# Guard rows issued by ScalarE, operand loads two to a chunk, value products dealt two-one-one, and fewer filler products

## The reference

```python
q, k, v = proj(Wq, bq), proj(Wk, bk), proj(Wv, bv)      # (16, 16 heads, 512, 8)
idx = clip(pos[None, :] - pos[:, None], -20, 20) + 20
attn1 = einsum('bhqd,bhkd->bhqk', q, k)
attn2 = einsum('bhqd,qkd->bhqk', q, rel_k[idx])
attn = softmax((attn1 + attn2) / sqrt(8), axis=-1)
w1 = einsum('bhqk,bhkd->bhqd', attn, v)
w2 = einsum('bhqk,qkd->bhqd', attn, rel_v[idx])
out = (w1 + w2) @ Wo.T + bo                              # heads merged
h = silu(norm(x) @ wg.T) * (norm(x) @ wu.T); y = x + h @ wd.T
```

## Time and profile before

| | |
|---|---|
| median of 3 runs | 1243.12 us (1238.39 to 1249.95) |
| the profiled execution | 1245.63 us, its span 1243.6 us |
| PE busy | 1182.3 us, 95% of the span |
| DVE, ACT, POOL busy | 938.9, 711.7, 578.2 us |
| mean granted clock of TensorE | 0.992 of full speed |
| attention stage, first row pair to last scores | 121.7 to 1075 us of the span |

### The profile page before, as it was taken

The page is one execution under the profiler, slowest core; times in us unless marked ns, Lnnn a source line. Parts: engine busy times, 40 slices in busy tenths (PEclk is TensorE's granted clock), DMA queues, the critical chain, the costliest instruction groups (busy, mean ns, idle before and its releaser), DMA issues. The chain is left out here.

```text
span 1243.6 us, 58027 instructions
## 1 busy us (share of the span) xinstructions
PE 1182.3 (95%) x25941; PEld 805.3 (65%) x25954; DVE 938.9 (75%) x1811; ACT 711.7 (57%) x1334; POOL 578.2 (46%) x1083
## 2 busy tenths in 40 slices
PE   5888999999999999999999999999999999999998
PEld 3555366666666666666666666666666666766675
DVE  7897777787787777777777787878887777266664
ACT  6876256666666566556666666666666666622222
POOL 5986655454445444544435454444454544122321
PEclk9999999999999999999999999999999999999999
DMA  5776201111112020202021211111111200022321
GB/s 170 228 226 209 65 4 30 51 42 38 50 34 61 19 68 13 70 9 71 16 65 30 59 36 52 48 40 54 34 53 31 67 14 9 9 72 86 94 77 51
DMA packets 92799, 76.37 MB, mean 61 GB/s; under 512 B 12744, under 2 KB 88328, under 8 KB 92552
## 3 DMA queue, kind: packets, MB, share of 16 engines
q1 hardware_dynamic: 92552, 72.67, 20.2%
HBM read 44.86 MB, written 26.21 MB: 57 GB/s over the span
## 5 line engine op out<-in xcount | busy, mean ns | idle before, releaser
L1161 DVE TENSOR_REDUCE b_mx<-b_a 128x1 f32<-128x512 f32 x1024 | 656.2, 682 | 188.0 <-PE b_a L877 187.6
L1125 ACT ACTIVATE b_p<-b_s 128x512 f32<-128x512 f32 x1024 | 569.7, 595 | 367.0 <-PE b_s L936 229.1
L823 POOL TENSOR_TENSOR qd<-q,one 48x512 bf16<-48x512 bf16 x256 | 266.2, 1040 | 252.4 <-PE b_s L936 233.2
L992 PE MATMUL b_pv<-b_p,vg 128*32 128x256 f32 x4096 | 276.9, 384 | 0.0
L936 PE MATMUL b_s<-qd,z 112*128 112x32 bf16 (+1 forms) x6016 | 248.6, 189 | 0.3
L877 PE MATMUL b_a<-k,q 48*128 48x512 bf16 x1024 | 199.7, 386 | 17.7 <-DMA q<-b_mt 9.8
L936 PEld LDWEIGHTS b_s<-qd,z 112*128 112x128 bf16 (+1 forms) x6016 | 204.2, 98 | 10.3 <-issue 0.6
L898 PE MATMUL b_s<-q,k 54*128 54x64 bf16 (+5 forms) x4096 | 186.4, 206 | 10.6 <-ACT b_p L1125 8.2
L898 PEld LDWEIGHTS b_s<-q,k 54*128 54x128 bf16 (+1 forms) x4096 | 111.6, 95 | 106.5 <-ACT b_p L1125 37.9
L992 PEld LDWEIGHTS b_pv<-b_p,vg 128*32 128x32 f32 x4096 | 116.2, 109 | 59.9 <-issue 20.4
L802 POOL TENSOR_TENSOR b_np<-b_db,one 128x16 bf16<-128x16 bf16 x192 | 39.1, 267 | 222.7 <-issue 186.5
(11 more groups left out here) (139 smaller groups left out, 1210.3 us busy)
## 6 DMA issues: line engine op xcount, KB each, us to landing
x<-in_x SPq DMA_DIRECT2D x24, 256.0 KB, 3.3
scratch_qop<-a_parts SPq DMA_DIRECT2D x16, 384.0 KB, 2.6
scratch_kop<-a_parts SPq DMA_DIRECT2D x16, 384.0 KB, 3.4
k<-scratch_kop SPq DMA_DIRECT2D x32, 192.0 KB
q<-scratch_qop SPq DMA_DIRECT2D x32, 192.0 KB
scratch_v<-a_vr SPq DMA_DIRECT2D x16, 256.0 KB, 3.5
k<-scratch_kop SPq DMA_DIRECT2D x32, 128.0 KB
q<-scratch_qop SPq DMA_DIRECT2D x32, 128.0 KB
```

Of the source, the lines that this page charges most:

```text
L823: nc.gpsimd.tensor_tensor(dst, src, one, ALU.mult).then_inc(s["qd_ready"], 1)
L992: nc.tensor.matmul(PV[V32 * a:V32 * (a + 1), g * PT:(g + 1) * PT], v[:, side, half, t, 2 * a + g, :], PR[pos][:, 4 * a + 2 * half + g, :], ...
L1125: nc.scalar.activation(out, src, ACT.Exp, scale=SCALE).then_inc(s["p_ready"], 1)
L1161: nc.vector.tensor_reduce(MX[unit.v % 2][:, h:h + 1], PA[(HP * n + hp) % NBANK][:, :], AX_X, ALU.max, negate=True).then_inc(s["a_used"], 1)
```

## The change

Four things are changed, all in `stage_attend`.

- The two transfers of the guard rows are issued by ACT instead of SP, right behind ACT's copy, with a wait on that copy's own semaphore. At the head of the stage ACT also waits for the stores of stage two, as SP does.
- SP issues the operand transfers two to a chunk in chunks 0 to 5 (`PIECES`), and the values in chunk 7 instead of 12.
- The first key block's value products of a pair are dealt as two groups, one, one over chunks 10, 11, 12; they were one, two, one. In chunks 4, 5 and 12 to 15 the row pair is put ahead of the wait for a score bank; it stood behind it.
- Behind each of the first four row pairs stand two filler products instead of four.

```diff
--- before.py
+++ after.py
@@ -37,6 +37,7 @@
 K_LOAD = ((0, 0, 3), (3, 0, 2), (5, 0, 1))
 Q_LOAD = ((0, 0, 3), (3, 1, 2), (5, 2, 1))
 NLOAD = 2 * (len(K_LOAD) + len(Q_LOAD))
+PIECES = ((0, 1), (2, 3), (4, 5), (6, 7), (8, 9), (10, 11))
 PARTS = 3
 OPR = SLOTS * HD
 HALF = 64
@@ -720,13 +721,6 @@
     with nc.Block() as block:
         @block.sync
         def _(sp):
-            def guard_rows(unit):
-
-                sp.wait_ge(s["mt_copied"], unit.v + 1)
-                for hp in range(HP):
-                    sp.dma_start(Q[unit.p][HALF * hp + GROW:HALF * hp + ROWS, :, hp, unit.i * P:(unit.i + 1) * P],
-                                 MT[hp * 6 * HH:(hp + 1) * 6 * HH, :]).then_inc(s["m_in"], 16)
-
             def store(pair):
 
                 sp.wait_ge(s["norm"], pair + 1)
@@ -736,7 +730,6 @@
             for p in range(ORING):
                 sp.wait_ge(k["stored"][p], 16 * NOUT * len(range(p, B, ORING)))
             load_score_operands(sp, k, d, 1, 1, range(9))
-            guard_rows(Unit(0))
             load_score_operands(sp, k, d, 1, 1, range(9, NLOAD))
             load_values(sp, k, d, 1, 1)
 
@@ -744,18 +737,14 @@
                 batch = pair // 2
                 ahead = pair % 2 == 0 and 0 < batch < B - 1
                 for c in range(CHUNKS):
-                    if ahead and c < NLOAD:
+                    if ahead and c < len(PIECES):
                         sp.wait_ge(s["s_ready"], PB2 * pair + 2 * c + 1)
-                        load_score_operands(sp, k, d, batch + 1, (batch + 1) % 2, [c])
-                    if ahead and c == NLOAD:
+                        load_score_operands(sp, k, d, batch + 1, (batch + 1) % 2, PIECES[c])
+                    if ahead and c == len(PIECES) + 1:
                         sp.wait_ge(s["s_ready"], PB2 * pair + 2 * c + 1)
                         load_values(sp, k, d, batch + 1, (batch + 1) % 2)
-                    if c == second_guard(pair):
-                        guard_rows(Unit(2 * pair + 1))
                     if c == 11 and pair:
                         store(pair - 1)
-                    if c == first_guard(pair) + 1 and pair < LAST:
-                        guard_rows(Unit(2 * pair + 2))
                 if pair == 8:
                     for p in range(2):
                         sp.wait_ge(xo_out[p], 32)
@@ -949,8 +938,8 @@
 
                 e, pos, g = CHUNK[c]
                 if pos == 3:
+                    row_pairs_ahead(pair, c)
                     wait_bank(pair, c, 1)
-                    row_pairs_ahead(pair, c)
                     side_by_side([far_scores_of_both(pair, c, hp) for hp in range(HP)]).then_inc(s["s_ready"], 2)
                     return
                 unit = Unit(2 * pair + e)
@@ -965,9 +954,10 @@
                         diagonal_scores(pair, c, unit, n)
                         relative_scores(pair, c, unit, n).then_inc(s["s_ready"], 1)
                     return
+                if c not in BESIDE:
+                    row_pairs_ahead(pair, c)
                 wait_bank(pair, c, 1)
                 if c not in BESIDE:
-                    row_pairs_ahead(pair, c)
                     side_by_side([far_scores(pair, c, hp) for hp in range(HP)]).then_inc(s["s_ready"], 2)
                     return
                 side_by_side([beside_scores(pair, c, hp, hp, True) for hp in range(HP)]).then_inc(s["half"], 1)
@@ -1060,7 +1050,7 @@
 
             for n in range(FIRST):
                 row_pair(n)
-                keep_busy(4)
+                keep_busy(2 if n < 4 else 4)
                 if n == HH + 1:
                     pe.wait_ge(s["init"], 1)
                     guard_transpose(Unit(0))
@@ -1084,7 +1074,7 @@
                     if c == first_guard(pair) and pair < LAST:
                         guard_transpose(Unit(2 * pair + 2))
                     if c in (10, 11, 12):
-                        value_products(pair, 0, ((0,), (1, 2), (3,))[c - 10])
+                        value_products(pair, 0, ((0, 1), (2,), (3,))[c - 10])
                     if c >= 12:
                         value_products(pair, 1 + (c - 12) // 2, range(2 * (c % 2), 2 * (c % 2) + 2))
                     if pair and c in (13, 14, 15):
@@ -1129,11 +1119,17 @@
                 if unit.v:
                     act.wait_ge(s["m_in"], 32 * unit.v)
                 nc.scalar.copy(MT[:, :], MI[0:6 * H, 0:P]).then_inc(s["mt_copied"], 1)
+                act.wait_ge(s["mt_copied"], unit.v + 1)
+                for hp in range(HP):
+                    nc.scalar.dma_start(Q[unit.p][HALF * hp + GROW:HALF * hp + ROWS, :, hp, unit.i * P:(unit.i + 1) * P],
+                                        MT[hp * 6 * HH:(hp + 1) * 6 * HH, :]).then_inc(s["m_in"], 16)
 
             def first_rows():
                 act.wait_ge(o["xT"], 1)
                 nc.scalar.copy(XNT[:, :], PA[2][:, :]).then_inc(o["xTs"], 1)
 
+            for p in range(ORING):
+                act.wait_ge(k["stored"][p], 16 * NOUT * len(range(p, B, ORING)))
             guard_copy(Unit(0))
             for pair in range(PAIRS):
                 for c in range(CHUNKS):
```

## The result

| | before | changed |
|---|---|---|
| median, 4 runs each on one chip | 1243.69 us (1238.39 to 1249.95) | 1328.32 us (1325.84 to 1332.18) |
| span of the profiled execution | 1243.6 us | 1323.7 us |
| mean granted clock | 0.992 | 0.957 |

The ratio is 1.068, with an interval of 1.065 to 1.071: **6.8% slower**, outside the predicted range of 1226 to 1260 us. Slower by over 1% had the chance 0.28. The two mechanisms that were priced for it, a collision of issues and a dear issue, are not the cause; a wait at chunk 6 was named beside them, at no more than 14 us.

A forecast was written before the change was run, and what follows sets the result against it. PE, busy for 95% of the span, was taken to bound the kernel. The terms -9.1 + 20 - 6 - 2.3 = +2.6 us on the median of 1243.12 gave 1246 us, with 1226 to 1260 for 8 in 10.

The forecast's parts named there:

- a collision of issues: Rival: SP's and ACT's issues in chunks 2 and 3 shut each other out, 12 us in 14 pairs, 1258 us; chance 0.2.
- a dear issue: Rival: an issue costs ACT 0.96 us, more than SP, so 32 + 10 us instead of 20, 1268 us; chance 0.08.
- SP's pairing and ACT's wait at the head cost nothing: Loads two to a chunk and ACT's wait for stores at the stage's head: 0, operands being wanted in the next pair.
- the signs that the prediction set: ACT's DMA rows 0.7 to 0.8 us, `q<-b_mt` waits some 2 us, 0.6 us waits at chunk 4, none at chunk 11.
- The rival at chunk 6: Guard rows late at chunk 6 with twice the operands in flight: 1 us in 14 pairs, 14 us; no separate chance.
- Chunk 0, -9.1 us: Pair starts: with the values five chunks earlier, guard rows land sooner and PE's waits go, 9.1 us gained.
- the cited rule: The Trainium skill's rule: a second issuing engine saves only issue time, since all transfers interleave on the same 16 DMA engines.
- ACT's issue in chunk 2, +20 us: ACT's two guard-row issues delay chunk 3's exponentials, so chunk 4's scores start 0.64 us late in 31 pairs: 20 us lost.
- the formula: Loss for a pair at chunk 4: twice ACT's issue minus 0.88 us, nothing below 0.44 us an issue.
- Chunk 12: 0: ACT's two issues after its copy there delay chunk 13's exponentials, but a cover of 0.1 us makes the cost 0.
- Deal and hoist, -6 us: Chunks 10 to 12: value products two, one, one and the earlier row pair gain 0.2 us in each of 31 pairs.
- Fillers, -2.3 us: First four row pairs, at half clock: two fillers less in each interval bring unit 0's guard rows earlier, 2.3 us gained.

The follow-up runs named there:

- one load a chunk: The changed kernel with operand transfers again one to a chunk in chunks 0 to 11 and the values in chunk 12: 1265.55 us, ratio 1.016.
- the kernel without that step: The kernel before with value products two, one, one, the hoisted row pair and two fillers behind the first four row pairs: ratio 0.997 to the kernel before.
- ACT's queue alone: The kernel before with only the guard rows' issue moved to ACT, and ACT's wait for the stores at the head: 1279.89 us, ratio 1.028.

## Why the prediction was wrong, point by point

- **The step that failed:** "SP's pairing and ACT's wait at the head cost nothing: the operands are wanted in the next pair". True of the operands, but not of what is in flight beside them. The runs show in its place a landing of 8.7 us instead of 2.9 and 47.5 us of waits at chunk 6; undoing the pairing takes back 63 of 85 us (one load a chunk against the changed kernel). I asked when the moved transfers are needed and not which small urgent transfer stands in their stream. Of the signs that the prediction set, those on ACT's issue held (741 ns, and 0.55 us at chunk 4); the one that failed is PE's waits for `q<-b_mt`, 55.2 us instead of some 2. The rows to see it in were at hand: the argument for chunk 0 says that 320 KB of values ahead of the guard rows make them late, and twice the operands around chunk 2's guard rows is the same kind of case.
- **The rival at chunk 6** had the right mechanism and the wrong size. I compared the 3 us from the issue's end to chunk 6 with no landing time. From the first issue to chunk 6 (273.88) they are 4.5 us, and an undisturbed landing takes 2.9 from there: a room of 1.6 us. With the backlog it took 9.2 us. A wait of 1 us in 14 pairs was assumed; it was 3.4 us at the mean. It had no price for the half clock behind each wait, most of PE's 29.6 us of longer busy time, and no chance of its own.
- **The head of the stage** wasn't free either, though ACT's wait for the stores, which the same step names, is not what costs: ACT's copy there waited for PE's transpose until 134.99 us. The guard rows of the first unit stood in SP's queue ahead of the last three q loads of the second batch; these now go out before them. PE waits 6.8 us instead of the 0.71 of the earlier trace rows, and the fillers' 2.3 us are lost in it.
- **Chunk 0, -9.1 us:** right in size, and the reason only in part. These waits are gone, and values behind the guard rows alone took some 10 us off the kernel without that step (1240.95 to 1230.97), of which PE's waits for guard rows name 5.8. But the values made 0.6 us of a landing of 6.6, and q's last transfers the greater part; and ACT's queue alone takes the same waits away with the values in their old place. So the sentence that by the cited rule the gain comes from the values' place and not from ACT's queue is wrong. The values' place by itself took 8.9 us of waits to 3.1, ACT's queue by itself took all but the first pair's, and its landing of 5.0 us beside 6.2 is more than issue time saved.
- **ACT's issue in chunk 2, +20 us:** right, a little high. 17.1 us in 31 waits is 0.55 us a pair beside 0.64; without the hoist it is 0.81, and the formula (0.60 with the median issue, plus the 0.23 between row pair and scores in the earlier trace rows) gives 0.83. Chunk 12: 0, right.
- **Deal and hoist, -6 us:** right, 6.1 us. **Fillers, -2.3 us:** the prediction's own terms (0.86, 0.86 and 0.79) add up to 2.5. Measured are 1.55 us at the place and 0.8 us in the time, not told from 0.
- **The issues collide, or are dear:** neither. ACT's issue took 741 ns at the median, and so did the 30 of its 128 issues that overlapped one of SP's. The Trainium skill (Perfetto Trace Analysis, "DMA Instruction — HWDGE (DVE, Sync)") has issues wait for a shared generator; these 30 show no such wait at the median (the longest is 1.63 us). SP's own issues did become long, up to 4.33 us, in this kernel, and do so in the kernel with ACT issuing nothing in this stretch too (6.99 us for three of q at 410.92 us with the guard rows on SP), so that goes with the backlog and not with two queues.

## What to carry to other kernels

When transfers are moved earlier or closer together, look for the small transfer that somebody waits for and that now stands among them; its price is how long what surrounds it takes to land, not its own bytes. Before packing issues, work out how fast the moved transfers drain: here twelve loads needed about the twelve chunks that they had. And add to a wait of several microseconds of TensorE the stretch behind it that runs at half clock, which here was about half as much again (22 us beside 47.5).

## What the runs showed of the hardware

- Two transfers of 12 KB landed 2.9 us after their first issue with idle queues. As medians of 14 pairs it was 5.7 us with six transfers of k ahead, 7.2 with four of q ahead and two beside, and 8.7 and 9.4 with three of q on either side, from ACT's and from SP's queue. In the changed kernel the DMA share was no more than 0.23 in the windows in which PE waited for them: a low share does not say that a transfer will be quick.
- k and q move the same bytes into as many rows, yet q in front costs 28.2 us of waits and k 8.1, and guard rows issued about four chunks behind them land in 6.4 us behind q and 2.9 behind k. Cutting q into 8-row transfers took the changed kernel's waits at chunk 6 from 48.4 to 19.1 us, and added 70 packets under 512 bytes a batch.
- With loads in SP's queue, guard rows from ACT's queue landed sooner than from SP's in two places: 8.7 instead of 9.4 us at chunk 2 of the changed kernel, 5.0 instead of 6.2 at chunk 12 of the kernel before. But with ACT's queue the loads also come closer: at chunk 2 of the kernel before, 2.9 us became 5.8.
- An issue on SP, 0.70 to 0.76 us at the median, grew to as much as 4.33 us when much was in flight.
- With PE still for 1.3 and 1.7 us the granted clock stayed at 1.00; with waits of 2.4, 4.0 and 6.6 us it fell to 0.50 (1.2 GHz) and stayed there for 4 us or more of full work.
- An issue of the same transfer costs ACT what it costs SP, 741 and 740 ns.
